# Two chunks' diagonal products in one stretch: a state space mixer with a LoRA layer on one core

## The reference

```
proj = x @ in_proj_w.T                  -> gate (8192), hs|B|C (8192+1024+1024), dt (128)
hs, B, C = silu(causal_conv4(hs|B|C)) ; dt = clip(softplus(dt + dt_bias), 0, 100)
x_dt = hs * dt                          (128 heads of 64, 8 groups, chunks of 128 tokens)
Y_diag[l] = sum_{s<=l} (C_l . B_s) * exp(Acum_l - Acum_s) * x_dt[s]      inside a chunk
state     = decay * state + sum_s B_s * exp(Acum_last - Acum_s) * x_dt[s]   chunk to chunk
Y_off[l]  = C_l . state_before * exp(Acum_l)
g = (Y_diag + Y_off + hs * D) * silu(gate) ; g = g * rsqrt(mean over group(g^2) + eps) * norm_w
x1 = layernorm(x + g @ out_proj_w.T) ; out = layernorm(x1 + (x1 @ W.T + bias + LoRA(x1)))
```

## Time and profile before

| what | value |
|---|---|
| median of three runs | 1571.26 us |
| the profiled execution, its span | 1572.33 us, 1570.5 us |
| granted TensorE clock, mean | 0.996 |
| TensorE busy | 1540.6 us (98%), 8664 matmuls |
| VectorE, ScalarE, GpSimd busy | 1354.5 (86%), 1209.6 (77%), 1335.6 us (85%) |
| DMA | 229.04 MB, mean 146 GB/s |

### The profile page before, as it was taken

One profiled execution on the slowest core, in us unless ns is written; L12 is line 12 of the kernel. 1 busy time (PEld: TensorE's weight loads), 2 busy tenths in 40 slices (PEclk: granted clock), 3 DMA queues, 4 the chain that ended last, 5 costly groups with the idle time before them and its releaser, 6 DMA issues.

```text
span 1570.5 us, 27374 instructions
## 1 busy us (share of the span) xinstructions
PE 1540.6 (98%) x8664; PEld 1259.0 (80%) x8664; DVE 1354.5 (86%) x1878; ACT 1209.6 (77%) x2360; POOL 1335.6 (85%) x1124
## 2 busy tenths in 40 slices
PE   8999999999999999999999999999999999999998
PEld 6878888887888878888788878888888887888765
DVE  6778898888989799897989889897898879988797
ACT  5888778886878877887877877878777886778864
POOL 4489789897998979998899988999799897999974
PEclk9999999999999999999999999999999999999999
DMA  3655444544454443545355444454435445364431
GB/s 118 214 184 162 158 123 150 168 143 130 128 175 155 125 151 126 181 135 152 125 154 162 131 148 135 139 179 141 134 128 172 151 122 157 115 189 141 166 104 61
DMA packets 164190, 229.04 MB, mean 146 GB/s; under 512 B 25040, under 2 KB 86480, under 8 KB 163792
## 3 DMA queue, kind: packets, MB, share of 16 engines
q1 hardware_dynamic: 163040, 227.14, 46.4%
q10 hardware_dynamic: 1008, 0.17, 0.1%
HBM read 193.14 MB, written 34.08 MB: 145 GB/s over the span
## 4 chain that ended last, share of the span: by engine, by line
PE 59%; POOL 16%; issue 9%; DVE 8%; ACT 5%; DMA 2%; ACTq 0%; SPq 0%; POOLq 0%; DVEq 0%
PE proj L560 10%; PE proj L562 10%; PE proj L561 10%; PE p_out L608 5%; PE p_out L610 5%; PE p_out L609 5%; PE p_yd L736 5%; PE p_st L617 4%; POOL w_lo L1080 2%; POOL xd L1116 2%; POOL dh L1160 2%; DMA raw<-w_t 2%; POOL xd_lo L1120 2%; ACT decay L890 2%; DVE bT L1276 2%
## 5 line engine op out<-in xcount | busy, mean ns | idle before, releaser
L560 PE MATMUL proj<-x_hi,w_hi 128*128 128x512 f32 x1160 | 463.6, 400 | 9.2 <-DVE x_lo L1410 6.9
L562 PE MATMUL proj<-x_hi,w_lo 128*128 128x512 f32 x1160 | 453.8, 391 | 0.0
L561 PE MATMUL proj<-x_lo,w_hi 128*128 128x512 f32 x1160 | 453.7, 391 | 0.0
L890 ACT ACTIVATE decay<-decay,tok 128x128 f32<-128x128 f32 x1024 | 312.6, 391 | 0.0
L1276 DVE SCALAR_TENSOR_TENSOR hs<-proj,uch,hs 128x511 f32<-128x511 f32 (+2 forms) x384 | 283.5, 738 | 29.3 <-ACT hs L829 24.2
L1080 POOL TENSOR_TENSOR w_lo<-raw,w_hi 128x512 fp32r<-128x512 f32 x177 | 251.4, 1420 | 40.1 <-ACT w_hi L802 33.2
L560 PEld LDWEIGHTS proj<-x_hi,w_hi 128*128 128x128 f32 x1160 | 219.4, 189 | 53.8 <-issue 8.8
L562 PEld LDWEIGHTS proj<-x_hi,w_lo 128*128 128x128 f32 x1160 | 218.7, 189 | 46.3
L561 PEld LDWEIGHTS proj<-x_lo,w_hi 128*128 128x128 f32 x1160 | 219.4, 189 | 42.1
L1314 DVE TENSOR_TENSOR decay<-decay,cb 128x1024 f32<-128x1024 f32 x128 | 209.8, 1639 | 46.5 <-ACT decay L908 46.4
L1160 POOL TENSOR_TENSOR dh<-dh,eac 128x512 f32<-128x512 f32 x96 | 131.0, 1365 | 99.2 <-DVE eac L1345 96.6
(11 more groups left out here) (143 smaller groups left out, 3024.3 us busy)
## 6 DMA issues: line engine op xcount, KB each, us to landing
decay<-acum_d SPq DMA_DIRECT2D x128, 512.0 KB, 4.4
raw<-w_t SPq DMA_DIRECT2D x177, 256.0 KB, 2.8
turned_d<-x_blk SPq DMA_DIRECT2D x112, 256.0 KB, 2.0
x_tok_sb<-turned_d SPq DMA_DIRECT2D x448, 64.0 KB, 1.9
eac<-eacum_d SPq DMA_DIRECT2D x192, 128.0 KB, 3.1
wo_raw<-wo_t SPq DMA_DIRECT2D x32, 256.0 KB, 3.5
c_new<-wo_t SPq DMA_DIRECT2D x32, 256.0 KB, 4.3
hs<-x_t SPq DMA_DIRECT2D x8, 256.0 KB, 5.3
```

The costliest lines, as they stand in the source:

```text
L560: nc.tensor.matmul(dst[:], w_hi[:, ws, k, :], x_hi[:, k, cols], start=(k == 0), stop=False)
L561: nc.tensor.matmul(dst[:], w_hi[:, ws, k, :], x_lo[:, k, cols], start=False, stop=False)
L562: mm = nc.tensor.matmul(dst[:], w_lo[:, ws, k, :], x_hi[:, k, cols], start=False, stop=(k == KC - 1))
L890: ins = nc.scalar.activation(decay[:, dslot(c), h, :], decay[:, dslot(c), h, :], ACT.Relu, scale=-1.0, bias=tok[:, e, 0, c, h:h + 1])
```

## The change

The two diagonal blocks of an even step and of the odd step behind it run one after the other in the even step. The odd one goes to the bank `p_hid`, which until now held only the turned hs of chunk 0. For that, `xdt` has two buffers, `decay` four slots (`c % 4`), C two (`cT`, by the group's parity, instead of `c_new` and `cT`), all four tiles of output weights have a buffer of their own (`wo_raw`), and the transposes go straight to `x_tok_sb` (the buffer `x_blk` is gone). Group 0 keeps its first two blocks apart.

`front` runs two steps ahead instead of one: in even steps behind the pair, in odd ones behind `project_out`. The turning of hs of chunk 0 (`first_tokens`) stands at the end of chunk 7's step and waits for all y of its unit. Store and load of the turned blocks are three steps ahead instead of two, `scale_tokens` up to two. On ScalarE, GpSimd and VectorE the `body` is replaced by three lists, `first_unit(g)`, `second_unit(g)` and `last_unit(g)`, in which every instruction stands by name.

```diff
+        def diagonals(g, e, c):
+            if (g, e) == (0, 0) and c < 2:
+                return [c]
+            return [] if c % 2 else [c, c + 1]
+        def prepared(g, e, c, last):
+            o, e2, c2 = ahead(e, c, 2)
+            return [] if last and o else [(g + o, e2, c2)]
         def load_decay(q, g, e, c):
-            wait(q, yd_ready, step(g, e, c) - (1 if c % 2 else 3))
+            wait(q, yd_ready, 0 if step(g, e, c) < DECAYS else step(g, e, c) - (DECAYS - 1))
         # load_blocks
-                wait(sp, xdt_ready, step(g, e, c) - 1)
+                wait(sp, xdt_ready, n - 2)
         # TensorE
+            def first_tokens(g, e):
+                u = 2 * g + e
+                wait(pe, y_ready, 8 * u)
+                pe.wait_ge(hs_ready, 8 * u + (7 if u else 4))
+                for j in range(UT):
+                    mm = nc.tensor.transpose(p_hid[:, j, :], hs[:, e, j, 0:P], ident[:])
+                mm.then_inc(hid_ready, 1)
+            def diagonal(g, e, c):
+                s = step(g, e, c)
+                dst = p_hid if c % 2 else p_yd
+                wait_xdt(pe, g, e, c)
+                pe.wait_ge(mix_ready, s + 1)
+                wait(pe, y_ready, s - 1)
+                for h in range(UH):
+                    mm = nc.tensor.matmul(dst[(h % 2) * HD:(h % 2 + 1) * HD, h // 2, :],
+                                          xdt[:, c % 2, h, :], decay[:, dslot(c), h, :], start=True, stop=True)
+                mm.then_inc(yd_ready, 1)
         # body, behind the first tile and norm_sum
-                        (wait for xdt, mix and y of the step before; eight products into p_yd; front of the next step)
+                        for x in diagonals(g, e, c):
+                            diagonal(g, e, x)
+                        ahead_of = prepared(g, e, c, last)
+                        if c % 2 == 0:
+                            for x in ahead_of:
+                                front(*x)
...
         # body, behind project_out
+                        if c % 2:
+                            for x in ahead_of:
+                                front(*x)
+                        off, ne, _ = after(e, c)
+                        if c == 7 and not (last and off):
+                            first_tokens(g + off, ne)
         # VectorE, turn_blocks
-                wait(dve, blocks_stored, 16 * (turn_n(g, e, c) - 1))
+                wait(dve, xdt_ready, n - 2)
-                nc.vector.transpose(x_blk[:], hs[:, e, :, c * P:(c + 1) * P].rearrange("p j (q a) -> p q j a", q=UT)
+                nc.vector.transpose(x_tok_sb[:, n % 2], hs[:, e, :, c * P:(c + 1) * P].rearrange("p j (q a) -> p q j a", q=UT)
```

More of the change, by code:

```diff
@@ L506, in body @@
                             load_eac(sp, g + o1, e1, c1)
[L507 removed]
+                        od, ed, cd = ahead(e, c, DECAYS)
                         if not (last and od):
                             load_decay(sp, g + od, ed, cd)
[L510 to L512 removed]
+                        blocks = turned(g, e, c, last)
+                        if blocks:
+                            store_blocks(*blocks[0])
                         tiles = tiles_of(e, c, last)
@@ L730, in body @@
                             norm_sum(g - 1, 6 + c, False)
-                        pe.wait_ge(xdt_ready, s + 1)
-                        pe.wait_ge(mix_ready, s + 1)
-                        wait(pe, y_ready, s)
-                        for h in range(UH):
-                            mm = nc.tensor.matmul(p_yd[(h % 2) * HD:(h % 2 + 1) * HD, h // 2, :],
-                                                  xdt[:, h, :], decay[:, dslot(c), h, :], start=True, stop=True)
-                        mm.then_inc(yd_ready, 1)
-                        off, ne, ncn = after(e, c)
-                        if not (last and off):
-                            front(g + off, ne, ncn)
+                        for x in diagonals(g, e, c):
[4 more added lines that the diff above has]
+                                front(*x)
                         if (e, c) == (0, 6):
@@ L1063, in _ @@
+            for g in range(GROUPS):
+                first_unit(g)
+                if g < G:
+                    second_unit(g)
+                else:
+                    last_unit(g)
             copy_turned(5)
@@ L1570, in _, with total @@
-            groups(body)
+            turn_blocks(0, 0, 2)
+            high_tokens(0, 1)
+            products(0, 1)
+            def total(g, e, c):
+                s = step(g, e, c)
+                dve.wait_ge(yd_ready, s + 1)
+                dve.wait_ge(dh_ready, s + 1)
+                wait(dve, ghi_ready, s)
+                wait(dve, sq_ready, s)
+                wait(dve, glo_ready, s)
+                nc.vector.tensor_tensor(y[:], (p_hid if c % 2 else p_yd)[:], dh[:], ALU.add).then_inc(y_ready, 1)
@@ new lines, in square_sum @@
+            def square_sum(g, e, c, last=False):
+                if e and not last:
+                    dve.wait_ge(sqt_ready, 8 * g + c + 1)
+                else:
+                    dve.wait_ge(sq_ready, step(g, e, c) + 1)
+                if e == 0:
+                    wait(dve, var_ready, 8 * g - 7 + c)
+                nc.vector.tensor_reduce(last_sqs(c) if last else sqs[:, c, :], ysq[:].rearrange("p a b -> p b a"),
+                                        AX.X, ALU.add).then_inc(sqs_ready, 1)
@@ new lines, in last_unit @@
+            def last_unit(g):
+                for c in range(8):
+                    s = step(g, 1, c)
+                    if c == 7:
+                        take_var(g, 5)
+                    if c == 1:
+                        wo_split_lo(g, 1, (2, 3))
+                    total(g, 1, c)
+                    if 1 < c < 7:
+                        take_var(g, c - 2)
+                    if c % CPB != CPB - 1:
+                        state_sum(g, 1, c)
+                    if c < 5:
+                        turn_blocks(g, 1, c + 3)
+                    if c < 6:
+                        mix(g, 1, c + 2)
+                    if c > 1:
+                        add_normed(g, c - 2)
+                    lns = [(w, c - (2, 5)[w]) for w in range(2) if c >= (2, 5)[w]]
+                    if c in (1, 2, 4, 5, 6):
+                        scale_off(g, 1, c + 1)
+                    if c == 7:
+                        ln_begin(0, 5)
+                        lns = lns[1:]
+                    for ln in lns:
+                        ln_stats_1(*ln)
+                    for ln in lns:
+                        ln_stats_2(*ln)
+                    square_sum(g, 1, c, True)
+                    for ln in lns:
+                        ln_stats_3(*ln)
+                    if c >= 4:
+                        add_ffn(c - 4)
+                    if c > 0:
+                        add_out(g, c - 1)
+                    if c == 7:
+                        take_var(g, 6)
+                    if c == 0:
+                        wo_split_lo(g, 1, (0, 1))
+                        scale_off(g, 1, 1)
+                    if c == 3:
+                        fold_weight(2)
+                        fold_weight(3)
+                    low_gated(s)
+                    if c == 2:
+                        fold_weight(0)
+                        fold_weight(1)
```

1076 lines of the change are left out of this document (723 added, 353 removed).

## The result

The changed kernel takes 1593.1 us (median of 4 runs, 1591.4 to 1594.2), the kernel before 1570.6: ratio 1.0142 [1.0124, 1.0159]. It is slower by 22.6 us; the forecast was 1563. The profiled execution has a span of 1592.0.

What follows compares the result with a forecast made beforehand. TensorE was taken to bound the kernel (185.5 of 186.8 us per group). Terms -6.3 - 10.1 - 0.5 + 1.5 + 6 + 1 = -8.4 us gave 1563 us, own range 1559 to 1568, 8-in-10 range 1555 to 1574.

Steps and rivals of the forecast that it cites:

- SP's queue: SP's loads and stores: loads start earlier, transposes come one step sooner; nothing, up to 1 us per group in the bound.
- Pairs on TensorE: Paired diagonal blocks save entry prices of 0.09 us and few exits: -6.3 us over eight groups, bounds 0 and 10.9.
- Two steady waits gone: Waits at carried_out of (1,3) and the state product of (1,4) both go: -10.1 us, bounds 0 and 11.3.
- Rival C: Pair brings what it says, but waits come back elsewhere: about 1572 us, no change; chance 0.14.
- Group 0: Group 0's start: transpose ahead of total(0,0) makes the state late, carried_out waits 4.6 us; +6 us, bounds 0 and 9.
- first_tokens: Chunk 7's first_tokens must wait for total before a projection on TensorE: 0.1 us per unit, 1.5 us in all.
- rival B: Second bank: first_tokens waits 0.9 us for VectorE fifteen times, with slow clock +8.4 us, 1580 us; chance 0.16.
- The last unit: Last unit: pairs need mix and scale_tokens a step sooner, small waits; +1 us, bounds -5 and +6.5.
- Clock: A 4 us wait in group 0 can bring half clock, mostly hidden by ScalarE's list; some included in group 0's +6.

Runs made afterwards that it cites:

- e16_queue_apart: e15_queue_g0 with each pair of diagonal blocks taken apart, the odd block behind the state product: 1581.7 us.
- e15_queue_g0: e12_queue with group 0's transpose turn_blocks(0,0,3) moved behind state_sum(0,0,0) on VectorE: 1562.6 us.
- e12_queue: e7_store plus, in SP's queue, the store ahead of eac and decay in (1,2) and the block load ahead of the weight tiles in (0,3): 1562.9 us.
- e6_apart: e5_lists with each pair of diagonal blocks taken apart, the odd block behind the state product: 1598.4 us.
- e3_start: Changed kernel with, only in group 0, the transpose turn_blocks(0,0,3) behind state_sum(0,0,0) instead of ahead of total(0,0,0): 1591.9 us.
- e7_store: Changed kernel with, in step (g,0,2) alone, SP's store of turned blocks (0,5) ahead of the eac and decay loads: 1569.6 us.
- e2_sp: Changed kernel with SP's queue reordered in every step: decay load, store, eac load, block load, then weight tiles: 1616.7 us.
- e5_lists: Changed kernel with VectorE's late state_sum and scale_off instructions moved up, decay_state(g,0,6) up on GpSimd, and group 0's start reordered: 1594.1 us.
- e9_fit: e7_store with two add_normed sums moved to step (0,1), some state and scale_off instructions moved up, group 0's transpose later: 1579.9 us.

## Why the prediction was wrong, step by step

The medians divide the difference. Before 1570.5; with the change's orders but the blocks apart and the queue mended 1581.7 (e16_queue_apart), so **+11** for the orders; the pairs **-19** (1562.6, e15_queue_g0); the queue as the change has it **+30** (1593.1 against 1562.9, e12_queue, three places of the queue). Some 6 of the +11 may be TensorE's own stream: taken apart, the odd block stands behind the state product and not where it stood before, and the stream is 1520.0 in e6_apart against 1514.0 before. What the rest is was not separated.

- **SP's queue** is the step that failed. The prediction put it at "nothing, up to 1 us per group", because the loads start earlier and the transpose is asked for and given one step sooner. Both are true, and they are the reason: the transpose comes so early now that the store no longer waits for it, but for the eac load ahead of it, which hangs on add_carried, at the old time. The tokens were needed a step sooner and came hardly sooner. Measured: 30 us, 23.5 of it by the one store of (0,5). I looked at the waits inside the store and not at those of the commands ahead of it in the same queue.
- **Pairs on TensorE** (-6.3) was mis-sized: 17 us in the stream, 19 us in the time (e16_queue_apart against e15_queue_g0), outside even the bound of 10.9. The entry of 0.09 was read rightly. The exit was read from the distance behind the small products that follow, and missed 0.1 us inside the block's own 1.02. A distance from a block's start to the next kind holds its drain; only two equal blocks in a row show it.
- **Two steady waits gone** (-10.1): right, both are gone in the trace after. But the estimate of 2.7 us and more of room elsewhere came from adding up lists that had their inputs on time; (0,5), at 1.3 to 4.0 us, is no place that the prediction named. Rival C was its kind (the waits come back elsewhere), at 1572.
- **Group 0**, +6: the wait at carried_out is 6.8 us (4.6 predicted), because the four loads went out at 71.1 and not 68.4, and diag(0,0,2) started at 100.1 (99.5 predicted). That this wait is mostly hidden by what follows was right as well: e3_start took it away and won nothing that can be told. But it is not ScalarE's list alone that bounds the start, as ScalarE waited 2.4 us for gate_y there.
- **first_tokens (rival B)**: 0.5 us in four units. Priced at 1.5 in all, measured 2.0; B as a cause is refuted. (Its own threshold was off: 8.4 + 3.1 + 1.5 less 2.4 is 10.6, over fifteen 0.7 us and not 1.)
- **The last unit**, +1: its waits of 1.2, 2.7 and 2.1 us stand where small ones were expected. Yet from its first diagonal block to the end of the span it is 103.8 us after (from 1488.17) and 105.6 before (from 1464.96), 1.7 less. Its four pairs are worth 1.2 of that at 0.3 each, so the +1 did not come.
- **Clock**: expected once, in group 0; it came behind each wait of 3 us or more inside the kernel, six times, 1.5 to 2.9 us each, 12 us in all, and once more in the last unit, behind waits of 2.7 and 2.1 us. Before, it came in group 0 too (80.9 to 84.3), which the prediction did not see.
- The sum came out at what e12_queue measures (1563) by luck, two errors that cancel: the pair 13 us too small, all the rest (-2 forecast, +11 measured) 13 us too cheap.

VectorE's room was the other wrong reading behind it: 88% busy was taken as 22 us of slack per group to be had anywhere. In e7_store it is 96% in steps (0,4) to (0,7) and 65% right behind.

## What to carry to other kernels

- When producer and consumer of a transfer are both moved earlier, move the command that starts it as well: read the queue it stands in, and what each command ahead of it waits for. Here one store, moved ahead of two loads in one step of sixteen, was worth 23.5 us, and a new order of the same queue in every step (e2_sp) cost 23.6; the order has to follow the times at which things are ready, step by step.
- A saving on the bounding engine shows in the time only where the others' lists have room. The same pair was worth -4, 4, 9, 17 and 19 us in five kernels. Measure an edit with the late waits mended, not on top of them.
- In a stretch where an in-order engine has no idle time, moving one instruction up can make another late (e5_lists, e9_fit). Look at its busy share by stretch, not over the whole.

## What the runs showed of the hardware

- Two diagonal blocks (16 products each, 64 columns wide) in a row start 0.92 us apart. What follows a block that stands alone starts 1.02 us behind it, what follows the second of a pair 0.98. In the sum a block alone pays 0.3 us that the second of a pair does not (19.5 us over 63 pairs). The drain of a change of mode, for which the prediction cited the Trainium skill ("TensorEngine Tiling (Array Packing)", Key Properties), fits this, at about 0.1 on entry and 0.2 at the end; no run here tells a drain from another cost of the same size.
- In the changed kernel the clock was 1.2 GHz behind each wait of 3.1 us and more. That is no rule: in e15_queue_g0 the granted clock stayed 1.00 behind one of 3.57 us (at 86.2), and in the kernel before it was 0.50 from 80.9 to 84.3, behind two waits of only 0.8 us each (at 78.7 and 80.4). Behind waits of 2.0 to 2.5 us it fell in some groups and not in others of the same kernel (e5_lists: one of 2.03 us cost 2.3, another of 2.03 cost 3.9). Equal waits have unequal prices. e7_store's runs spread over 13 us, where 18 runs of the kernel before spread over 3 and seven others over 5.5; whether the clock is the reason was not tested.
- Instructions of one form do not take one time: g_lo took 0.68 to 1.78 us in the changed kernel and dh 1.0 to 2.0. In the rows of e5_lists the long ones of VectorE and GpSimd run side by side. That they stretch each other is inferred from this, and was not tested.
- A 256 KB store took 2.0 us from issue to landing in the kernel before (median), 4.3 after. Where no decay load was under way when it was issued (16 of 112 stores) it took 2.1 after as well, and 4.4 beside one (96 stores). So the queue order seems to cost twice, once in SP and once in the transfer.
